# A four-layer kernel on one core: in the second attention, q and k projected with the weights stationary, their halves exchanged and stacked by DMA

## What is computed

```
def _L1_attn_ref(x, W_in, b_in, W_out, b_out):      # H = 16 heads, KD = VD = 64, D = 256
    proj = x @ W_in.T + b_in                        # x is the layer-normed input
    q, k, v = proj[..., :1024], proj[..., 1024:2048], proj[..., 2048:]   # each to (b, 16, 512, 64)
    q, k = _rope(q, sin, cos), _rope(k, sin, cos)
    att = einsum('bhqd,bhkd->bhqk', q, k) / 8, causal mask, softmax
    y = einsum('bhqk,bhkd->bhqd', att, v)
    return y.reshape(b, t, 1024) @ W_out.T + b_out

def _rope(x, sin, cos):                             # x_hi, x_lo: first and last 32 of the 64 columns
    y_lo = x_lo * cos + x_hi * sin
    y_hi = x_hi * cos - x_lo * sin
    return concatenate([y_lo, y_hi])
```

## Time and profile before

| | us |
|---|---|
| median of 3 runs (2305.91 to 2318.0) | 2306.05 |
| the profiled execution | 2315.66 |
| its span, first to last instruction | 2313.9 |

### The profile page before, as it was taken

How to read it: one execution, slowest core, us unless ns; L and a number is a source line. 1 busy time by engine, 2 the same in 40 slices (tenths; PEclk the granted TensorE clock), 3 DMA queues, 4 the chain that set the end, 5 groups by cost and what they waited for, 6 DMA issues and landing times. The chain is left out here.

```text
span 2313.9 us, 52728 instructions
## 1 busy us (share of the span) xinstructions
PE 1965.5 (85%) x18758; PEld 1405.2 (61%) x18759; DVE 1723.1 (74%) x3717; ACT 1398.9 (60%) x2736; POOL 1036.8 (45%) x1231
## 2 busy tenths in 40 slices
PE   2889989899862999378799999999999999549999
PEld 1666666666561666145577777676767777426665
DVE  4778888788791444468678787879696977679997
ACT  1666666666562444267668696868787878344443
POOL 4435534355014000488747576657575663132222
PEclk9999999999955999689999999999999999869999
DMA  7000000000033332002100000000000000100000
GB/s 241 2 1 2 2 2 2 2 2 2 3 128 127 98 91 79 12 11 35 22 1 2 2 2 2 2 1 2 1 2 2 2 2 2 38 1 14 18 18 23
DMA packets 53114, 57.77 MB, mean 25 GB/s; under 512 B 7121, under 2 KB 47217, under 8 KB 52897
## 3 DMA queue, kind: packets, MB, share of 16 engines
q1 hardware_dynamic: 46240, 45.00, 6.2%
q0 software_dynamic: 6656, 9.85, 2.0%
HBM read 36.22 MB, written 18.61 MB: 24 GB/s over the span
## 5 line engine op out<-in xcount | busy, mean ns | idle before, releaser
L371 PE MATMUL a_bank<-w_in_sb,xnT_sb 128*128 128x512 f16 x1152 | 293.7, 394 | 33.7 <-DVE t_buf_sb L579 26.4
L1116 DVE TENSOR_REDUCE neg_max_sb<-a_bank 128x1 f32<-128x128 f32 (+3 forms) x512 | 236.1, 485 | 92.6 <-PE a_bank L896 88.7
L531 DVE TENSOR_REDUCE neg_max_sb<-a_bank 128x1 f32<-128x128 f32 (+3 forms) x512 | 236.1, 482 | 92.6 <-PE a_bank L288 91.1
L1039 ACT ACTIVATE probT_sb<-a_bank 128x512 f32<-128x512 f32 (+1 forms) x384 | 198.8, 526 | 145.3 <-PE a_bank L919 140.5
L442 ACT ACTIVATE p_hi_sb<-a_bank 128x384 f16<-128x384 f32 (+1 forms) x384 | 205.3, 535 | 120.7 <-PE a_bank L297 119.0
L434 ACT ACTIVATE prob_sb<-a_bank,neg_max_sb 128x128 f32<-128x128 f32 (+3 forms) x512 | 261.4, 543 | 23.9 <-DVE neg_max_sb L531 23.0
L538 DVE TENSOR_TENSOR p_lo_sb<-a_bank,p_hi_sb 128x384 f16<-128x384 f32 (+1 forms) x384 | 228.0, 595 | 59.7 <-ACT p_hi_sb L442 56.1
L453 ACT ACTIVATE stack_sb<-a_bank 128x1024 f16<-128x1024 f16 (+1 forms) x256 | 211.4, 826 | 7.0 <-PE a_bank L342 6.6
L297 PE MATMUL a_bank<-ident_f_sb,prob_sb 128*128 128x128 f32 x1280 | 206.4, 276 | 3.7 <-DVE p_lo_sb L538 3.1
L707 POOL TENSOR_TENSOR rope_w_sb<-t_buf_sb,sin_sb 128x256 f32<-128x256 f32 x128 | 146.0, 1140 | 134.7 <-DVE t_buf_sb L579 132.2
L371 PEld LDWEIGHTS a_bank<-w_in_sb,xnT_sb 128*128 128x128 f16 x1152 | 104.9, 100 | 143.0 <-DVE t_buf_sb L579 34.2
(11 more groups left out here) (268 smaller groups left out, 5613.3 us busy)
## 6 DMA issues: line engine op xcount, KB each, us to landing
sorted_rows<-zeros_sb SPq DMA_DIRECT2D x1, 4992.0 KB, 21.6
x_in_sb<-sorted_rows SPq DMA_DIRECT2D x39, 128.0 KB, 2.1
sorted_results<-y_moe_sb SPq DMA_DIRECT2D x39, 128.0 KB, 1.7
x_sb_sb<-L_attn_x SPq DMA_DIRECT2D x8, 512.0 KB, 10.7
w_raw_sb<-L_ffn_gate_bank SPq DMA_DIRECT2D x8, 512.0 KB, 3.6
w_raw_sb<-L_ffn_up_bank SPq DMA_DIRECT2D x8, 512.0 KB, 4.7
w_raw_sb<-L_ffn_down_bank SPq DMA_DIRECT2D x8, 512.0 KB, 5.8
out<-x_sb_sb SPq DMA_DIRECT2D x32, 128.0 KB, 1.7
```

The costliest lines, as they stand in the source:

```text
L371: last = pe.matmul(out, xnT[:, x, c, j * P:(j + 1) * P], w["in"][:, w_, c, cols], start=k == 0, stop=k == len(terms) - 1)
L531: last = dve.tensor_reduce(neg_max[:, i:i + 1], S[(3 * h + g) % 2][:, off:off + L], AX.X, ALU.max, negate=True)
L1039: act.activation(probT[:, (h // 4) % 2, h % 4, T_AT[r]:T_AT[r + 1]], ST[(3 * h + r) % 2][:, 0:T_AT[r + 1] - T_AT[r]], ACT.Exp).then_inc(s_ ...
L1116: last = dve.tensor_reduce(neg_max[:, h % 2, i:i + 1], S[(3 * h + g) % 2][:, off:off + L], AX.X, ALU.max, negate=True)
```

## The change

It replaces `attention` by `attention1`.

- **q and k** are projected with the weights stationary, and all 512 tokens stream by: a *qk* fill gives the 128 columns of two heads (a *pair*) on partitions, with tokens along the row. q and k of a pair are one fill each, 16 a batch, six matmuls of 512 columns as before. So the head's columns already lie on partitions, and the stack transposes go, with their copies. v keeps its pieces (8 a batch).
- The two halves that RoPE exchanges now lie in *different partitions*. ACT copies the bank to `t_buf` (scale and bias in the same instruction), **SP issues four DMAs of 32 partitions by 2 KB** that exchange the halves into `t_swapped`, DVE multiplies the bank (bias added) by cos into `rope`, POOL multiplies `t_swapped` by sin and adds it to `rope`. ACT writes the high part `rope_hi`, POOL the low part `rope_lo`, both in a buffer of one for q and one for k.
- **SP issues the DMAs that stack the parts**: 4 of 64 partitions by 1 KB for q, 8 for k, into stacks of two pairs.
- SP's program is, for each pair in turn: swap q, swap k, stack q, stack k: 20 DMAs for a pair, 64 pairs.
- **The output projection** takes yT in fp16 parts (ACT the high, DVE the low part) against output weights in fp16 parts: 24 fp16 matmuls of 256 columns for a tile, in place of 8 in fp32. These weights are loaded and split at the head of the stage.
- The slots: pair p of a batch has its q fill in slot 6p-11 and its k fill in slot 6p-9 (negative ones in the batch before), and its scores from slot 6p on. POOL's rotation comes 2 slots behind the fill, ACT's high part 4, POOL's low part 5.
- The first attention's semaphores are cleared and given back behind it, with a barrier.

```diff
+AT1 = (tuple(6 * p - 11 for p in range(HEADS // 2)), tuple(6 * p - 9 for p in range(HEADS // 2)),
+       (5, 11, 14, 17), (29, 32, 35, 41), (20, 23, 26, 28), (55, 56, 57, 58), 1)
...
+    LAG_WA, LAG_WV, LAG_VH, LAG_VL, LAG_W, LAG_ZH, LAG_ZL = 0, 1, 3, 4, 2, 4, 5
...
+            elif kind == "qk":
+                t, p = a
+                wait(pe, s_xnT, (b + 1) * QT)
+                terms = [(x, w_, c) for x, w_ in TERMS for c in range(C)]
+                for n, (x, w_, c) in enumerate(terms):
+                    last = pe.matmul(out, w["in"][:, w_, c, t * 1024 + p * P:t * 1024 + (p + 1) * P], xnT[:, b % 2, x, c, :],
+                                     start=n == 0, stop=n == len(terms) - 1)
...
+                terms = [(y_, w_, c) for y_, w_ in TERMS for c in range(CHUNKS)]
+                for n, (y_, w_, c) in enumerate(terms):
+                    last = pe.matmul(out[:, 0:D], yT[:, y_, c, i * P:(i + 1) * P], w_out[:, w_, c, :],
+                                     start=n == 0, stop=n == len(terms) - 1)
...
+            elif kind == "qk":
+                wait(act, s_fill, n)
+                wait(act, s_sw[t], 16 * 4 * (unit(b, t, p) // 2))
+                act.activation(t_buf[:, t, :], W[bank][:, :], ACT.Identity, scale=1.0 / W1_SCALE,
+                               bias=w["bias_qk"][:, 0, t * PAIRS + p:t * PAIRS + p + 1]).then_inc(s_t, 1)
...
+        def rope_hi(b, t, p):
+            U = unit(b, t, p)
+            pr = U // 2 - 1
+            wait(act, s_z, U + 1)
+            if pr >= 0:
+                wait(act, (s_qs, s_ks)[t][pr % 2], 16 * (4, 8)[t] * (pr // 2 + 1))
+            act.activation(z_hi[:, t, :], rope[:, t, :], ACT.Copy).then_inc(s_zh, 1)
...
+        def rotate(b, t, p):
+            U = unit(b, t, p)
+            wait(pool, s_sw[t], 16 * 4 * (U // 2 + 1))
+            pool.tensor_tensor(t_sw[:, t, :], t_sw[:, t, :], w["sin"][:, t, :], ALU.mult).then_inc(s_w, 1)
+            wait(pool, s_u, U + 1)
+            wait(pool, s_w, U + 1)
+            pool.tensor_tensor(rope[:, t, :], rope[:, t, :], t_sw[:, t, :], ALU.add).then_inc(s_z, 1)
+
+        def rope_lo(b, t, p):
+            U = unit(b, t, p)
+            wait(pool, s_zh, U + 1)
+            pool.tensor_tensor(z_lo[:, t, :], rope[:, t, :], z_hi[:, t, :], ALU.subtract).then_inc(s_zl, 1)
...
+        def swap_halves(U):
+            t = U % 2
+            wait(sp, s_t, U + 1)
+            wait(sp, s_z, U - 1)
+            for r in range(0, P, 32):
+                src = r + 32 if r % 64 == 0 else r - 32
+                sp.dma_start(t_sw[r:r + 32, t, :], t_buf[src:src + 32, t, :]).then_inc(s_sw[t], 16)
+
+        def stack(pr, t):
+            U = 2 * pr + t
+            wait(sp, s_zl, U + 1)
+            wait(sp, s_scores, 6 * (pr - 1))
+            for a in range(2):
+                hi, lo = z_hi[a * DH:(a + 1) * DH, t, :], z_lo[a * DH:(a + 1) * DH, t, :]
+                if t == 0:
+                    sp.dma_start(q_st[0:DH, pr % 2, a, :], hi).then_inc(s_qs[pr % 2], 16)
+                    sp.dma_start(q_st[DH:P, pr % 2, a, :], lo).then_inc(s_qs[pr % 2], 16)
+                else:
+                    sp.dma_start(k_st[0:DH, pr % 2, 0, a, :], hi).then_inc(s_ks[pr % 2], 16)
+                    sp.dma_start(k_st[DH:P, pr % 2, 0, a, :], lo).then_inc(s_ks[pr % 2], 16)
+                    sp.dma_start(k_st[0:DH, pr % 2, 1, a, :], lo).then_inc(s_ks[pr % 2], 16)
+                    sp.dma_start(k_st[DH:P, pr % 2, 1, a, :], hi).then_inc(s_ks[pr % 2], 16)
+
+        for pr in range(B * PAIRS):
+            for t in range(2):
+                swap_halves(2 * pr + t)
+            for t in range(2):
+                stack(pr, t)
...
+            nc.clear_and_free_semaphores(a0_sems)
+            nc.all_engine_barrier()
```

1029 lines of the change are left out of this document (426 added, 603 removed).

## The result

| | before | changed |
|---|---|---|
| median of the runs, us | 2309.24 | 2587.26 |
| lowest and highest, us | | 2584.9 and 2591.73 |
| ratio, 95% interval | | 1.12, 1.116 to 1.124 |
| span of the profiled execution, us | 2313.9 | 2589.9 |
| PE, DVE, ACT, POOL busy, us | | 1960.5, 1665.5, 1266.5, 960.0 |

The forecast was 2382 us with a range of 2280 to 2440. The sign was right; the loss is 278 us where 76 were forecast, and the time lies far outside the range. Most of the fourteen experiments are about that difference. The kernel before had medians from 2309 to 2314 us beside them, so a few us between two experiments say nothing; each ratio is to the runs of before beside it.

A forecast was written before the change was run, and what follows sets the result against it. The prediction took PE to bound the kernel before, and waits through SP's DMA issues the changed one, at 133 us a batch for 122.9. Its terms, 5.5 + 61 + 17 - 8 + 1 = +76 on 2306, gave 2382 us, range 2280 to 2440.

The forecast's parts named there:

- the ring: Chain of waits through POOL's rotations and low part of q and 15 SP issues; 15.7 us a pair, 16.0 taken.
- What bounds before: Kernel before: PE sets the pace, busy 118.0 of 123 us a middle batch, some 5 us idle.
- part 1 and part 2: Engines' work a batch: PE falls from 118 to 104 us, ACT 96.9 to 75, DVE to some 93, POOL 77.4 to 67.
- the hidden rival: Narrow DMAs issue in 0.16 us, so PE sets the pace at 109 us a batch: 2192 us, chance 0.14.
- Part 3, the mechanism: SP's rigid DMA order delays POOL, then ACT's high parts and exponentials, then PE: 133 us a batch, 10.1 more.
- An issue at 0.48: Price of each DMA issue on SP's queue: 0.48 us, bounds 0.34 and 0.51, 15 of them a pair.
- Landing at 1.8: Time from a DMA's issue to its landing, for copies inside SBUF: 1.8 us, bounds 1.3 and 2.2.
- Coupling at 0.3: POOL's low part of a value delays that of q in two pairs of eight: 15.7 becomes 16.0 us a pair.
- the second ring: Chain through ACT's high part of k, k stacks, exchange and rotation: 11.7 us, 14.9 with ACT's other slots.
- One window of 21 us that PE sets: Slots 7 to 12 of a batch, with four output projections and one v piece: PE needs 21 us.
- Part 4: Ends and odd batches: first +5.5 us, six full +61, last +15 and +2, start -8, barrier +1.
- The clock: PE's halts bring the 1.2 GHz level, setting a pace of 19 us a pair: some 2500 us, chance 0.05.

The follow-up runs named there:

- e10_few: Changed kernel with 5 DMAs of all 128 partitions a pair instead of 20, both heads reading the first stack: 2257 us, ratio 0.972 to 0.979.
- e8_issues: Kernel before, with SP issuing 20 small DMAs a pair into a spare tile, none waited for by an engine: 2313.0 us, ratio 1.0004.
- e4_plus4: Changed kernel with four more DMAs a pair, into a tile nobody reads, issued with the k stacks: 2734 us, ratio 1.178 to 1.185.
- e3_k4: Changed kernel without four k-stack DMAs a pair; each score's second product rereads the first k stack: 2428 us, ratio 1.046 to 1.054.
- e13_heads: Changed kernel with three 128-row products a score, only high parts copied by DMA beside zeros, 12 DMAs a pair: 2289.0 us, ratio 0.989 to 0.993.
- e9_half: Changed kernel with each exchange and stacking DMA moving only 256 of its 512 columns, same number and order: 2573 us, ratio 1.111 to 1.118.
- e7_k6: Changed kernel with SP's stacks and exchanges alternating, low parts one slot earlier, six k stacks, second product of 64 rows: 2350 us, ratio 1.013 to 1.021.
- e11_nostack: Changed kernel without stacks: three 64-row products a score from ACT's and POOL's own tiles, 8 DMAs a pair: 2327 us, ratio 1.005 to 1.010.

## Why the prediction was wrong

The steps that failed are two terms of the ring's sum: the price of an issue, 0.48 us where 0.64 was measured, and the 0.3 us of coupling, where the mean pair lies 1.9 above the shortest. The mechanism held. With the measured issue and landing alone the prediction's sum would give 2382 + 54 x 2.6 = 2522 us; the last 65 are coupling and the first and last batch.

**What bounds before, part 1 and part 2** held. PE's work without the rings is 103 us a batch (forecast 104), DVE 93 and POOL 67 are as forecast, ACT has 80 for 75: the times of its instructions add up to 22.6 us less, as forecast (21.9), but neighbours overlap by 10 us a batch where they did by 16, which the sum left out. What failed there is the 5 us of PE's idle time carried over from before: e10_few has 13. It made the hidden rival 65 us too cheap and didn't bear on the forecast.

**Part 3, the mechanism** held: both rings exist as described, through SP's order, and every wait listed under what the profile would show is there. **Part 3, the terms** failed:

- *An issue at 0.48.* It is 0.64, outside the bounds of 0.34 and 0.51. On 15 issues that is +2.4 us a pair. The rows taken for it read from HBM, and e8_issues shows that for the same destination and size such issues are cheaper (0.43 against 0.60 busy). I had argued that the price doesn't follow the size, which is right, and took from it that it would follow nothing.
- *Landing at 1.8.* 2.0 in the median: +0.2. The longest are 4.0.
- *Coupling at 0.3.* The ring by the prediction's own steps is 15.7 + 2.4 + 0.2 = 18.3 with these prices, and 18.0 is the shortest seen. The mean is 19.9, so 1.6 to 1.9 lie above it. The table above says of what: the values' low parts, by which the prediction explained its 0.3 (1.2 us in two pairs of eight), measured 0.27. The rest had no term: pairs in which the second ring rules (its step from q's to k's high part 6.7 and 7.3 where the prediction had 3.8), long issues and landings, and waits around the rotations. Most often that step is 3.98, near the forecast.
- *One window of 21 us that PE sets.* This term held: the pair of 1360 takes 21.7 us in the mean of six and is still the longest. The other seven take 18.8 to 20.9, where 16.0 was forecast.

So a batch is 8 x 19.9 = 159, where 7 x 16.0 + 21 = 133 was forecast; of the 26 between them, 7 x 2.6 = 18 come from the two prices and nearly all the rest from the coupling.

**Part 4.** Six periods +220 instead of +61. The start is 16 us shorter (forecast 8, bounds 20 off and 5 on). The first batch loses 45 instead of 5.5: its eight rings are longer like all others, and the four pairs with POOL's indirect DMAs take 25.6, 25.6, 26.7 and 23.9 us, some 22 over four ordinary ones (forecast 19). The last one loses some 30 instead of 17.

**The rivals.** The clock was a rival of its own, 2500 us at 0.05. The clock did fall, to 0.86 in the middle, as a result of the halts, since with 5 DMAs a pair it is 0.99. But PE doesn't set a pace of 19, as that rival had it: it stands still for a quarter of the batch. The low clock shows where PE restarts behind a halt (2.76 us for 1.46), and of the 1.9 us of coupling it has about 0.2, by the steps compared above. That 2500 lies nearer to the measured time than the forecast is luck.

**The rule of the Trainium skill** that the prediction set against its own row stands in "DMA: Bandwidth & Descriptors", section Issuing engines are not separate DMA queues: the issue is usually small relative to the DMA itself. Here it isn't: 0.64 us in a burst beside a landing of 2.0, and 0.6 us for each DMA added or taken away (e4_plus4, e3_k4). The 50 ns with which the prediction made the ring hidden stand in that page's section Anatomy of one DMA — SWDGE (gpsimd) path, so for DMAs that GpSimd issues; those of SP are others, and the figure says nothing of them.

## What to carry to other kernels

Count the DMAs that one queue has to issue inside a loop of waits, and price each with a row of the same kind (for one, source and destination both in SBUF), since this ring paid for the issues and hardly for the bytes. When a hand-written order closes two rings, mending one shows little (64 and 21 us, together 192); find the second in the trace before judging the first. Split the mean turn of a ring into its steps and compare them with the shortest turn: that gave the 1.9 us of coupling term by term. A saving on the engine that bounds (here 15 us of PE a batch) is real only if what takes its place stays off the queue: e13_heads, with the same idea and 12 DMAs, turned +12% into -1%. No run here shares the DMAs out between two issuing engines, which is the obvious other way.

## What the runs showed of the hardware

- SP needs 0.59 to 0.60 us for an issue in a burst whose source is in SBUF and 0.43 for one from HBM (both into SBUF, e8_issues), with 0.04 between them; neither 32, 64 or 128 partitions nor 5 or 64 KB changed the former. The first of a burst takes 0.46 to 0.54.
- One issue in some 20 takes over 0.8 us, up to 2.0 (39 of 842 in the changed kernel).
- Landing hardly follows the bytes: 2.0 us for 64 KB inside SBUF, 1.8 to 1.9 for 32 KB (e9_half).
- PE loses 0.1 us at each change between products of 128 and of 64 rows (0.31 for 0.22 from start to start, e7_k6 and e11_nostack); among themselves products of 64 rows start as close as those of 128.
- 20 DMAs of 5 KB a pair beside PE, DVE, ACT and POOL don't lengthen the run (e8_issues, 1.0004).
